# Second attention stage: order of SyncE's transfers, place of the inversion of head sums, and scaling of results in one group

## The chip, the cores and the metric

The kernel runs on one core of a Trainium2 chip. The metric is device time in microseconds of one execution of the whole program, the median of several runs. TensorE (PE) multiplies matrices, VectorE (DVE), ScalarE (ACT) and GpSimd (POOL) compute elementwise, SyncE (SP) only issues transfers (DMAs) between HBM and the on-chip memory SBUF; PE writes to the accumulator memory PSUM.

## What is computed

Two transformer layers over x of 8 x 512 tokens with 256 features. Layer 0 adds an attention with softmax and a feed-forward network. Layer 1, the one at hand, adds a linear attention and a feed-forward network of 8 experts, of which each token takes 2:

```python
q = x @ Wq.T; k = x @ Wk.T; v = x @ Wv.T            # 16 heads of 16 features
q = elu(q) + 1.0
k = elu(k) + 1.0
kv_cumsum = cumsum(einsum('blhd,blhe->blhde', k, v), axis=1)
k_cumsum = cumsum(k, axis=1)
out = einsum('blhd,blhde->blhe', q, kv_cumsum)
normalizer = clip(einsum('blhd,blhd->blh', q, k_cumsum), 1e-06, None)
out = (out / normalizer[..., None]).reshape(b, l, HIDDEN) @ Wo.T
```

## The kernel before

Four stages run one after the other: `stage_f` and `stage_a` for layer 0, `stage_b` for the linear attention and the gating of layer 1, `stage_c` for the experts. All that follows is `stage_b`. Each engine has a program of its own, written by hand; engines wait for one another on counting semaphores, and the order on each engine is the order of its code.

The stage handles 8 batches (B = 8) of 512 tokens, each in 4 tiles of 128 tokens (t = 0 to 3). The loop over b on every engine is a software pipeline: in pass b the scores, masks and states of batch b are made, the queries, keys and values of batch b+1 (`make(b + 1, t)`: t=0 the transposed input, t=1 the queries, t=2 the keys, t=3 values, gates and expert choice), and the results of batch b-1 are scaled, projected and added. Pass 7 makes nothing new, pass 8 only finishes batch 7.

On DVE, in each tile of a pass: `mask(b, t)` (L1632) takes the scores from PSUM, `take_state(b, t)` (L1646) the new part of the state; then come the `make` parts: `x_low` (L1617), `feature("q")` and `feature("k")` (L1624), `weigh_experts` and `choose`. A feature needs PE's product and ScalarE's exponential (`b_ex`, L1786), and it frees a PSUM bank. PE, ACT and DVE hand the two banks `pG` from use to use in a fixed sequence, and in it `project_out(b-1, 0)` takes the bank of the first key feature and `project_out(b-1, 1)` that of the second.

The normalizer comes as a row of ones beside the values: the results `o` hold sums of heads in rows 16, 48, 80 and 112. To invert them on all partitions they go on a round trip through HBM, all from SP's queue: the sums from `o` to `dens` (L1396), `dens` to the tile `den` (128 x 64, L1398), DVE's `invert` (clamp L1652, reciprocal L1654), `den` to `invs` (L1400), and `invs` four times to `inv_rows` (L1405). `normalise(b, t)` (L1659), called a scaling below, multiplies a tile of `o` by a tile of `inv_rows`, both in SBUF. `project_out` (PE, L1537) needs it; `add_out` (DVE, L1664) adds the product to `x_t`, and SP stores `x_t` when the last `add_out` of the batch is done (`store`, L1410). `x_t` has 4 buffers, so `load(b + 2)` (L1390) waits until `store(b - 2)` has landed. SP issues transfers in the order of its code and stands still at each wait.

GpSimd in each pass: `add_state(b, 1)`, then `own_queries(b + 1)` (L1880, four operations TENSOR_SCALAR as soon as the query features are there), `add_state(b, 2)` (L1889), and between them the sends of rows to the experts (L1924). At the end of the stage it splits a first set of expert weights in four pieces (L1950), behind its last sends.

Of the kernel before, what the change touches and what calls it, by code (L numbers as in the profile page):

```python
# [34 lines left out]
B, S, D = 8, 512, 256  # L35
T = B * S
NT = S // P
# [100 lines left out]
def tokens(ap, b):  # L138

    return ap[bass.ds(b * S, S), :].rearrange("(t p) d -> p t d", p=P)  # L140
# [1084 lines left out]
def stage_b(nc, wq_t, wk_t, wvg_t, wo_t, bg, own2_d, causal_d, blocks_d, before_d, ident_d,  # L1225
# [11 lines left out]
    with ExitStack() as ctx:  # L1237
# [142 lines left out]
        def wait_read(eng, *what):  # L1380
            n = rounds[what]
            eng.wait_ge(round_read[n % 2], n // 2 + 1)

        with nc.Block() as block:
            @block.sync
            def _(sp):
# [2 lines left out]
                        sp.wait_ge(stored[b % RX], 16 * (b // RX))  # L1389
                    sp.dma_start(x_t[:, b % RX, :, :], tokens(x1, b)).then_inc(x_in[b % RX], 16)  # L1390

                def invert(b):


                    sp.wait_ge(o_out, NT * (b + 1))
                    sp.dma_start(dens[b % 2, :, :], o[16:P:32, b % 2, :, :].rearrange("j g q -> j (g q)")).then_inc(den_out, 16)  # L1396
                    sp.wait_ge(den_out, 16 * (b + 1))
                    sp.dma_start(den[:], dens[b % 2, :, :].rearrange("j (r e) -> (j r) e", e=64)).then_inc(den_in, 16)  # L1398
                    sp.wait_ge(inv_step, 2 * b + 2)
# [8 lines left out]
                def store(b):  # L1408
                    wait_read(sp, "out", b, NT - 1)
                    sp.dma_start(tokens(out, b), x_t[:, b % RX, :, :]).then_inc(stored[b % RX], 16)  # L1410
# [9 lines left out]
                load(1)  # L1420
                sp.dma_start(dispatch.raw[:], weights[0:P, :]).then_inc(dispatched, 16)
                for b in range(B + 1):
                    if b + 2 < B:
                        load(b + 2)
                    if b >= 1:
                        invert(b - 1)
                        if b == B:
                            store(b - 2)
                        if b != B - 1:
                            store(b - 1)  # L1430
                sp.wait_ge(dispatched, 16)
                sp.wait_ge(padded, 16 * (NE + 1))
                for i in range(RX):
# [154 lines left out]
            def _(dve):  # L1588
# [148 lines left out]
                for b in range(B + 1):  # L1737
                    for t in range(NT):
# [4 lines left out]
                        if t == 3 and b + 2 < B:  # L1743
                            norm(b + 2)
                        if b >= 1:
                            if t == 1:
                                invert(b - 1)
                            if t == 2:
                                for i in range(NT // 2):
                                    normalise(b - 1, i)  # L1750
                        if b + 1 < B:
                            make(b + 1, t)
                        if b >= 1 and t == 2:
                            for i in range(NT // 2, NT):
                                normalise(b - 1, i)
                        if b == B - 1 and t == 3:
                            count_tiles()
                        if b >= 1 and t >= 2:
# [615 lines left out]
```

## Time and profile before

| | us |
|---|---|
| median of 3 runs | 2083.79 |
| lowest, highest | 2082.50, 2087.86 |
| the profiled execution | 2079.97 |
| its span, first to last instruction | 2078.3 |
| PE, DVE, ACT, POOL busy | 1882.9, 1244.4, 931.8, 1270.1 |
| second attention, about | 1247 to 1600 |

The profile is that of one execution. A timeline row gives start, duration, engine, line, operation, tiles written and read; in brackets stands how long the engine idled before it and what ended the idle time. "x2" means that two such instructions in a row are shown as one. Matrix products of one line appear as many instructions, and ends on PE are modelled.

### The profile page before, as it was taken

The numbers are of one execution on the slowest core, as the hardware profiler recorded it, in microseconds if no ns is written. First come the engines' busy times: TensorE is split into PE (matmuls) and PEld (weight loads), VectorE is DVE, ScalarE is ACT, GpSimd is POOL, SyncE is SP. The second block draws the span as 40 slices with busy tenths as digits, with TensorE's granted clock in tenths as the row PEclk, the third lists the DMA queues.
The fourth block names the chain that finished last, engine by engine and source line by source line (L and its number), as shares of the span: only waits on it lengthen the run. The fifth ranks groups of instructions, "written<-read, shape, count | busy, mean of one in ns | idle before, by whom it ended". The sixth has DMA issues, their size and how long they took to land. (4 is left out here: it accounts for less than half of the span.)

```text
span 2078.3 us, 35394 instructions
## 1 busy us (share of the span) xinstructions
PE 1882.9 (91%) x12820; PEld 1311.8 (63%) x12820; DVE 1244.4 (60%) x1819; ACT 931.8 (45%) x1605; POOL 1270.1 (61%) x824
## 2 busy tenths in 40 slices
PE   6997799999999999999999976888883899998998
PEld 5887444544545454454544545676762899998998
DVE  5775466656565666656666525776763566656343
ACT  5885344334343433434334224433320456776554
POOL 3553588778687887868778643455463664435433
PEclk8999799999999999999999988999996899999999
DMA  4223322232231323213232202132224443332222
GB/s 138 102 107 113 107 58 64 50 96 62 72 82 31 92 62 84 62 38 92 52 102 52 62 32 105 41 96 68 72 67 148 133 86 81 85 77 53 37 47 42
DMA packets 82432, 158.35 MB, mean 76 GB/s; under 512 B 14680, under 2 KB 64088, under 8 KB 76496
## 3 DMA queue, kind: packets, MB, share of 16 engines
q1 hardware_dynamic: 64832, 130.50, 22.6%
q0 software_dynamic: 14592, 18.40, 5.6%
q10 hardware_dynamic: 2880, 7.73, 1.0%
q8 instruction: 82, 1.34, 0.3%
q14 instruction: 46, 0.38, 0.1%
HBM read 80.45 MB, written 44.15 MB: 60 GB/s over the span
## 5 line engine op out<-in xcount | busy, mean ns | idle before, releaser
L1162 ACT ACTIVATE a_pr<-a_pT 128x1024 f32<-128x1024 f32 x256 | 261.8, 1023 | 425.3 <-PE a_pT L940 425.3
L1195 POOL TENSOR_TENSOR a_total<-a_total,a_pr 128x1024 f32<-128x1024 f32 x128 | 320.6, 2505 | 148.9 <-ACT a_pr L1162 148.5
L1051 DVE TENSOR_REDUCE a_row_max<-a_pG 128x2 f32<-128x1024 f32 x256 | 309.1, 1220 | 144.6 <-PE a_pG L914 144.3
L953 PE MATMUL a_pA<-a_pr,a_v 128*64 128x512 f32 x1024 | 277.4, 620 | 0.1
L2154 DVE TENSOR_TENSOR c_h_lo<-c_h,c_h_hi 128x256 fp32r<-128x256 f32 x288 | 151.3, 532 | 181.3 <-ACT c_h_hi L2128 181.0
L2128 ACT ACTIVATE c_h<-c_pU,c_b_c 128x256 f32<-128x256 f32 x288 | 140.8, 489 | 177.9 <-PE c_pU L105 176.6
L1195 POOL TENSOR_TENSOR a_total<-a_pr 128x1024 f32<-128x1024 f32 x64 | 151.7, 2370 | 51.4 <-ACT a_pr L1162 51.1
L1176 POOL TENSOR_TENSOR a_by_cos<-a_by_cos,a_swapped 128x1024 f32<-128x1024 f32 x64 | 155.4, 2429 | 36.7 <-DMA a_swapped<-a_by_sin 36.6
L1183 POOL TENSOR_TENSOR a_qk_lo<-a_by_cos,a_qk_hi 128x1024 fp32r<-128x1024 f32 x64 | 158.7, 2480 | 2.3 <-ACT a_qk_hi L1130 2.3
L1045 DVE TENSOR_TENSOR a_by_sin<-a_pG,a_sin 128x1024 f32<-128x1024 f32 x64 | 78.3, 1224 | 129.4 <-PE a_pG L105 124.7
L2198 POOL DMA_INDIRECT out_x<-c_y,c_ids x72 | 118.0, 1639 | 40.8 <-DVE c_y L2168 24.1
L2128 ACT ACTIVATE c_h_hi<-c_pU,c_b_c 128x256 fp32r<-128x256 f32 x288 | 139.9, 486 | 0.0
L914 PEld LDWEIGHTS a_pG<-a_qk_hi 64*128 64x128 f32 x512 | 45.9, 186 | 143.7 <-issue 91.0
L914 PE MATMUL a_pG<-a_qk_hi 64*128 64x512 f32 x512 | 120.8, 489 | 5.1 <-ACT a_qk_hi L1130 3.8
L1130 ACT CAST a_qk_hi<-a_by_cos 128x1024 fp32r<-128x1024 f32 x64 | 67.0, 1046 | 110.3 <-POOL a_by_cos L1176 110.3
L103 PE MATMUL c_pU<-c_xT_hi,d_w_lo 128*128 128x256 f32 x368 | 108.8, 296 | 7.3 <-remote 6.2
L935 PE MATMUL a_pT<-a_qk_hi,a_qk_lo 64*128 64x512 f32 x512 | 113.2, 436 | 1.9 <-ACT a_pr L1162 1.7
L103 PE MATMUL c_pY<-d_w_hi,c_h_lo 128*128 128x256 f32 x368 | 105.5, 287 | 8.5 <-DVE c_h_lo L2154 8.3
L940 PE MATMUL a_pT<-a_neg_max,a_ones 64*128 64x512 f32 x512 | 108.9, 419 | 0.0
L104 PE MATMUL c_pU<-c_xT_lo,d_w_hi 128*128 128x256 f32 x368 | 106.7, 290 | 0.0
L105 PE MATMUL c_pU<-c_xT_hi,d_w_hi 128*128 128x256 f32 x368 | 105.9, 288 | 0.0
L953 PEld LDWEIGHTS a_pA<-a_pr,a_v 128*64 128x64 f32 x1024 | 50.8, 135 | 86.9 <-issue 85.9
(271 smaller groups left out, 4986.3 us busy)
## 6 DMA issues: line engine op xcount, KB each, us to landing
a_swapped<-a_by_sin SPq DMA_DIRECT2D x256, 128.0 KB, 2.3
a_inv_by_head<-mid_inverses SPq DMA_DIRECT2D x30, 512.0 KB, 5.8
c_x_t<-mid_rows SPq DMA_DIRECT2D x37, 272.0 KB, 2.9
mid_latents<-f_c_parts SPq DMA_DIRECT2D x8, 1024.0 KB, 3.9
a_latent_parts<-mid_latents SPq DMA_DIRECT2D x8, 1024.0 KB, 7.4
d_raw<-in_weights SPq DMA_DIRECT2D x3, 2048.0 KB, 8.2
c_raw<-in_weights SPq DMA_DIRECT2D x3, 2048.0 KB, 7.7
f_x_t<-in_x SPq DMA_DIRECT2D x8, 512.0 KB, 3.8
```

The costliest lines, as they stand in the source:

```text
L103: nc.tensor.matmul(out, l_lo, r_hi, start=start, stop=False, **kw)
L914: last = nc.tensor.matmul(pair[:, h, :], qk_hi[rows, u % RQ, 0, t * P:(t + 1) * P], qk_hi[rows, u % RQ, 1, :], start=True, stop=True)
L935: nc.tensor.matmul(pT[:, h, :], k[rows, 1, ks], q[rows, 0, :], start=(i == 0), stop=False)
L953: last = nc.tensor.matmul(pA[64 * h:64 * h + 64, :], v[:, t, p, h, :], pr[:, n % RP, h, :], start=(t == 0), stop=(t == NT - 1))
L1051: nc.vector.reduce_max(row_max[:, u % 2, :, t], pair[:], AX.X).then_inc(read, 1)
L1162: nc.scalar.activation(pr[:, n % RP, :, :], pT[:], ACT.Exp, scale=SCALE).then_inc(exp_done, 1)
L1176: nc.gpsimd.tensor_tensor(by_cos[:, u % 2, :, :], by_cos[:, u % 2, :, :], swapped[:], ALU.add).then_inc(rope_done, 1)
L1183: nc.gpsimd.tensor_tensor(qk_lo[:, u % RQ, :, :], by_cos[:, u % 2, :, :], qk_hi[:, u % RQ, :, :], ALU.subtract).then_inc(qk_lo_done, 1)
L1195: nc.gpsimd.tensor_tensor(total[:, u % 2, :, :], before, pr[:, n % RP, :, :], ALU.add).then_inc(summed, 1)
L2128: nc.scalar.activation(dst[:, m % RH, :], pU[m % RH][:], ACT.Relu, bias=b1_c[:, e, m:m + 1]).then_inc(relu_done[m % RH], 1)
L2154: nc.vector.tensor_tensor(h_lo[:, m % RH, :], h[:, m % RH, :], h_hi[:, m % RH, :], ALU.subtract).then_inc(h_lo_done[m % RH], 1)
L2198: pool.indirect_dma_start(out=out, out_offset=bass.IndirectOffsetOnAxis(ap=ids[:, t:t + 1], axis=0), in_=y[:, t, :], in_offset=None, compu ...
```

## The change

SP: the sending of sums becomes a function of its own, `send_sums`, and goes first in a pass; `store(b - 2)` follows it, then `invert(b - 1)`, then `load(b + 2)`. Before, a pass had `load(b + 2)`, the sums and `invert(b - 1)` together, then `store(b - 1)`. DVE: `invert(b - 1)` moves from t=1, ahead of the query features, to t=0, behind `x_low`; the four scalings of t=2 come in one group ahead of the key features, where two stood ahead of and two behind them. No instruction is added or taken out.

```diff
-                def invert(b):
-
+                def send_sums(b):
                     sp.wait_ge(o_out, NT * (b + 1))
                     sp.dma_start(dens[b % 2, :, :], o[16:P:32, b % 2, :, :]...).then_inc(den_out, 16)
+
+                def invert(b):
+
                     sp.wait_ge(den_out, 16 * (b + 1))
...
                 for b in range(B + 1):
+                    if b >= 1:
+                        send_sums(b - 1)
+                    if 2 <= b < B:
+                        store(b - 2)
+                    if b >= 1:
+                        invert(b - 1)
                     if b + 2 < B:
                         load(b + 2)
-                    if b >= 1:
-                        invert(b - 1)
-                        if b == B:
-                            store(b - 2)
-                        if b != B - 1:
-                            store(b - 1)
+                    if b == B:
+                        store(b - 2)
+                store(B - 1)
...
                         if b >= 1:
-                            if t == 1:
-                                invert(b - 1)
                             if t == 2:
-                                for i in range(NT // 2):
+                                for i in range(NT):
                                     normalise(b - 1, i)
                         if b + 1 < B:
                             make(b + 1, t)
-                        if b >= 1 and t == 2:
-                            for i in range(NT // 2, NT):
-                                normalise(b - 1, i)
+                        if b >= 1 and t == 0:
+                            invert(b - 1)
```

SP's queue in pass 3 before, from the load to the store at the pass's end:

```order
L1390 DMA b_x_t<-mid_x 128x4x256
L1396 DMA mid_dens<-b_o 4x2048
L1398 DMA b_den<-mid_dens 128x64
L1400 DMA mid_invs<-b_den 128x64
L1405 DMA b_inv_rows<-mid_invs 16x2048 x4
L1410 DMA out_x<-b_x_t 128x4x256
```

The same queue in pass 3 of the changed kernel (lines are 5 or fewer further down):

```order
L1395 DMA mid_dens<-b_o 4x2048
L1412 DMA out_x<-b_x_t 128x4x256
L1400 DMA b_den<-mid_dens 128x64
L1402 DMA mid_invs<-b_den 128x64
L1407 DMA b_inv_rows<-mid_invs 16x2048 x4
L1390 DMA b_x_t<-mid_x 128x4x256
```

The sums moved ahead of store and load, the store between the sums and the read of `den`, the load behind the inverse rows.

DVE's program in pass 3 before, from the first `take_state` to the end of t=2's `add_out`; `d_scores` is the mask's result, `b_state` and `b_part` are `take_state`'s:

```order
L1646 TENSOR_TENSOR b_state<-b_pS,b_blocks 128x512
L1617 TENSOR_TENSOR b_xT_lo<-b_pG,b_xT_hi 128x512 x2
L1632 TENSOR_TENSOR d_scores<-b_pA,b_causal 128x2048
L1646 TENSOR_TENSOR b_part<-b_pS,b_blocks 128x512
L1652 TENSOR_SCALAR b_den<-b_den 128x64
L1654 RECIPROCAL b_den<-b_den 128x64
L1624 SCALAR_TENSOR_TENSOR b_qT<-b_pG,b_ex 128x512 x2
L1632 TENSOR_TENSOR d_scores<-b_pA,b_causal 128x2048
L1646 TENSOR_TENSOR b_part<-b_pS,b_blocks 128x512
L1659 TENSOR_TENSOR b_o<-b_o,b_inv_rows 128x4x128 x2
L1624 SCALAR_TENSOR_TENSOR b_kT<-b_pG,b_ex 128x512 x2
L1659 TENSOR_TENSOR b_o<-b_o,b_inv_rows 128x4x128 x2
```

DVE's program at the same place of the changed kernel:

```order
L1651 TENSOR_TENSOR b_state<-b_pS,b_blocks 128x512
L1622 TENSOR_TENSOR b_xT_lo<-b_pG,b_xT_hi 128x512 x2
L1657 TENSOR_SCALAR b_den<-b_den 128x64
L1659 RECIPROCAL b_den<-b_den 128x64
L1637 TENSOR_TENSOR d_scores<-b_pA,b_causal 128x2048
L1651 TENSOR_TENSOR b_part<-b_pS,b_blocks 128x512
L1629 SCALAR_TENSOR_TENSOR b_qT<-b_pG,b_ex 128x512 x2
L1637 TENSOR_TENSOR d_scores<-b_pA,b_causal 128x2048
L1651 TENSOR_TENSOR b_part<-b_pS,b_blocks 128x512
L1664 TENSOR_TENSOR b_o<-b_o,b_inv_rows 128x4x128 x4
L1629 SCALAR_TENSOR_TENSOR b_kT<-b_pG,b_ex 128x512 x2
```

Clamp and reciprocal moved ahead of the mask of t=1, and the second pair of scalings ahead of the key features.

## Rows read from the trace of the kernel before

**Rows 1.** Table of stretches, pass 3: length, busy us (count) PE, PEld, DVE, ACT, POOL

```profile
1387.54:1424.93 37.39, 33.20 (x402) 26.28 (x401) 27.16 (x61) 13.82 (x29) 20.31 (x29) 1.00 0.29 76
```

**Rows 2.** Waits, 1353 to 1537 us: engine, who for whom, total, times, longest

```profile
PE b_pG L1537 <- DVE b_kT L1624: 14.0, 5, 3.5
```

**Rows 3.** Timeline of PE, pass 3 and pass 7: start, us, instruction, idle before

```profile
1397.84 1.15 PE L1487 MATMUL b_pA<-d_own,b_kT 32*128 32x256 f32 x16
...
1408.14 3.72 PE L1537 MATMUL b_pG<-b_wo,b_o 128*128 128x256 f32 x16 [2.62 <-DVE b_kT L1624]
...
1554.56 5.07 PE L1537 MATMUL b_pG<-b_wo,b_o 128*128 128x256 f32 x16 [4.58 <-DVE b_o L1659]
```

**Rows 4.** Timeline of DVE, pass 3, instructions apart

```profile
1392.17 2.29 DVE L1632 TENSOR_TENSOR d_scores<-b_pA,b_causal 128x2048 f32<-128x2048 f32 x1 [0.56 <-PE b_pA L1487]
...
1397.08 0.19 DVE L1652 TENSOR_SCALAR b_den<-b_den 128x64 f32<-128x64 f32 x1 [2.02 <-DMA b_den<-mid_dens]
...
1401.33 0.68 DVE L1646 TENSOR_TENSOR b_part<-b_pS,b_blocks 128x512 f32<-128x512 f32 x1
...
1405.77 1.11 DVE L1659 TENSOR_TENSOR b_o<-b_o,b_inv_rows 128x512 f32<-128x512 f32 x1 [3.76 <-DMA b_inv_rows<-mid_invs]
```

**Rows 5.** Timeline of SP's queue, passes 2 and 3, then passes 7 and 8

```profile
1387.65 0.40 SPq L1410 DMA_DIRECT2D out_x<-b_x_t  x1
...
1391.06 0.50 SPq L1396 DMA_DIRECT2D mid_dens<-b_o  x1
1395.21 0.34 SPq L1398 DMA_DIRECT2D b_den<-mid_dens  x1
1397.89 0.34 SPq L1400 DMA_DIRECT2D mid_invs<-b_den  x1
1399.37 2.33 SPq L1405 DMA_DIRECT2D b_inv_rows<-mid_invs  x4
...
1537.15 0.50 SPq L1396 DMA_DIRECT2D mid_dens<-b_o  x1
...
1546.88 3.32 SPq L1405 DMA_DIRECT2D b_inv_rows<-mid_invs  x4
1564.95 0.50 SPq L1396 DMA_DIRECT2D mid_dens<-b_o  x1
```

**Rows 6.** Timeline of ACT: last copy of batch 2's results; first key exponential

```profile
1382.80 0.57 ACT L1812 COPY b_o<-b_pO 128x512 f32<-128x512 f32 x1
...
1403.78 0.64 ACT L1786 ACTIVATE b_ex<-b_ex 128x512 f32<-128x512 f32 x1
```

**Rows 7.** Timeline of POOL, pass 3: own queries and `add_state`

```profile
1398.90 6.19 POOL L1880 TENSOR_SCALAR d_own<-b_qT,b_own 128x512 f32<-128x512 f32 x4
1405.07 1.26 POOL L1889 TENSOR_TENSOR b_state<-b_state,b_part 128x512 f32<-128x512 f32 x1
```

**Rows 8.** Timelines of DVE and POOL: scalings of passes 1, 6; first stage

```profile
1329.63 0.92 DVE L1659 TENSOR_TENSOR b_o<-b_o,b_inv_rows 128x512 f32<-128x512 f32 x1 [1.60 <-DMA b_inv_rows<-mid_invs]
1330.47 2.19 DVE L1659 TENSOR_TENSOR b_o<-b_o,b_inv_rows 128x512 f32<-128x512 f32 x1
...
1517.43 2.54 DVE L1659 TENSOR_TENSOR b_o<-b_o,b_inv_rows 128x512 f32<-128x512 f32 x1 [2.33 <-DMA b_inv_rows<-mid_invs]
...
77.89 1.19 POOL L338 TENSOR_SCALAR f_diag<-f_ident,f_rstd 128x128 f32<-128x128 f32 x1
78.61 0.77 DVE L528 TENSOR_TENSOR f_g_lo<-f_g,f_g_hi 128x512 fp32r<-128x512 f32 x1
```

**Rows 9.** Timelines of DVE, POOL and PE, passes 7 and 8

```profile
1553.72 2.63 DVE L1659 TENSOR_TENSOR b_o<-b_o,b_inv_rows 128x512 f32<-128x512 f32 x4 [4.37 <-DMA b_inv_rows<-mid_invs]
...
1567.45 9.23 POOL L1950 TENSOR_TENSOR d_w_lo<-d_raw,d_w_hi 128x1024 fp32r<-128x1024 f32 x4
...
1570.25 6.48 DVE L1652 TENSOR_SCALAR b_den<-b_den 128x64 f32<-128x64 f32 x1 [1.87 <-DMA b_den<-mid_dens]
...
1585.76 9.98 PE L1537 MATMUL b_pG<-b_wo,b_o 128*128 128x256 f32 x32 [17.84 <-DVE b_o L1659]
```

## The prediction

> **What bounds the kernel now.** I read the views from coarse to fine. The change touches only the second attention, from about 1247 to 1600 us. The table of stretches [rows 1] shows one pass of its loop, from the first mask of one batch to that of the next: 37.39 us with TensorE (PE) busy for 33.20 and VectorE (DVE) for 27.16. So PE bounds a pass, and some 4 us of it are not PE's. The view of waits over passes 2 to 6 [rows 2] names most of them: PE waited 14.0 us in five times for a key feature of DVE, 3.5 us the longest. I call the pass with loop value b "pass b"; pass 3 starts at 1387.54 us and stands for passes 2, 5 and 6.
>
> In pass 3 the timelines tell what is late. PE is idle for 2.62 us and starts `project_out(2,0)` at 1408.14 [rows 3], so it was free at 1405.52. That product needs the bank that the first key feature frees, and this feature stands on DVE behind two scalings of results (L1659), which wait 3.76 us for the inverse rows until 1405.77 [rows 4]. The rows are late because of SyncE: the sums were complete when ScalarE ended its copy at 1382.80 + 0.57 = 1383.4 [rows 6], but SP stood in `store(1)` until 1387.65, then waited with the next load for that store to land, and only then sent the sums, at 1391.06 [rows 5]. The other wait, 2.02 us before the clamp of `den` [rows 4], is on nobody's path: the mask behind it needs `scores(3,2)`, which PE ends at 1397.84 + 1.15 = 1398.99 [rows 3], later than DVE could be there.
>
> **SP's new order.** The sums go at about 1383.5. `store(1)` stays at 1387.65, since it waits for the last `add_out`. The read of `den` follows at 1388.1 instead of 1395.21, but behind 512 KB of store. A read alone needs 1.87 us (1395.21 to its use at 1397.08); the sums behind a load took 4.15 (1391.06 to 1395.21) [rows 4, 5]. So `den` lands between 1390.0 and 1392.3; I take the middle, 1391.1. The load of `x_t` goes behind the inverse rows, to about 1395.7. Its reader comes behind `project_out`, which ends at 1411.86 [rows 3] and would now end some 2.6 us earlier: 13 us of cover for one transfer, so it costs nothing. The last two stores keep their place.
>
> **Invert at t=0.** Clamp, reciprocal and SP's answer took 1397.89 - 1397.08 = 0.81 us. They go ahead of the mask of t=1 at 1392.17, where DVE idles 0.56 us for PE anyway [rows 4], from 1391.6 on. They delay that mask by 0.2 us, by 0.9 at the late bound of `den`. Queued behind it are `take_state` and through it GpSimd's `add_state` and own queries, which move by the same 0.2 us; `scores(3,2)` on PE needs the mask only at 1397.84. The inverses leave at 1392.4 instead of 1397.89, their rows 1.48 us later, at 1393.9 [rows 5]. Issue to use took 6.4 us here (1399.37 to 1405.77) and 6.8 in pass 7 (1546.88 to 1553.72) [rows 4, 5, 9]. So they are there by 1400.3 to 1401.4 with the late `den` too. DVE comes to use them after `take_state`, at 1401.33 + 0.68 = 1402.0 [rows 4]. The wait of 3.76 us goes.
>
> **Four scalings in one go.** Alone, four of them take 2.63 us [rows 9]: 1402.0 to 1404.6. The first exponential of the keys ends at 1404.42 [rows 6], its feature at 1405.3 with the 0.65 us that such an operation takes (2.63 / 4), and PE, free at 1405.52, waits for nothing: a gain of 2.6 us, the most there is. But the scalings now fall among GpSimd's four own queries (1398.90 to 1405.09) and its `add_state` (1405.07 to 1406.33) [rows 7], and a scaling reads two SBUF tiles. What that costs is the unknown of this change. The rows that bear on it: in pass 3 the first scaling met `add_state` and took 1.11 instead of some 0.68 us [rows 4]. In pass 1 one that started in the last own query took 0.92 and the next, which met `add_state`, 2.19; in pass 6 one that started in the last own query took 2.54, until `add_state` was over [rows 8]. In the first stage, where GpSimd runs four of the same kind of operation (TENSOR_SCALAR), a DVE operation with two SBUF inputs took 0.77 us, and it was GpSimd's that stretched, to 1.19 [rows 8]. I read this as: own queries let DVE in after 0.1 to 0.5 us, `add_state` does not. Then the four scalings pass before `add_state` with some 0.7 us of delay in all, the first key feature ends at 1402.0 + 2.6 + 0.7 + 0.65 = 1405.95, and PE gains 2.1 us instead of 2.6. Passes 2, 3, 5, 6: 4 x 2.1 = 8.4. Pass 4 lost 3.5 us in the same place [rows 2] and comes down to the same pattern: 3.0. In pass 1 the scalings come later among the own queries: 0.5. Together 11.9 us. After PE everything moves along, since DVE's chain of t=3 starts from `project_out`.
>
> **The end of the stage.** Pass 7 makes nothing new, so nothing covers its inverse rows: scalings at 1553.72, PE idle 4.58 us, `project_out` 5.07 us instead of 3.72 [rows 3, 9]. New: the read of `den` takes the place of the sums at 1537.15 [rows 5], lands by 1540.2, and the inverse rows leave at about 1542.8 instead of 1546.88. They land at 1549.4, and with some 1 us for the `add_state` of that pass the first scaling ends 3.3 us earlier than now. With the short idle PE's 16 products take 3.72 again, and the last copy of results comes 4.6 us earlier: the sums leave at 1560.3 instead of 1564.95. Here the gain grows. The clamp of the last batch takes 6.48 us now (1570.25 to 1576.7), the very time until GpSimd ends four splits of weights (1567.45 to 1576.68) [rows 9], and these do not move: they stand behind GpSimd's own sends. With the sums 4.6 us earlier the clamp comes at 1565.6, before the splits. The inverse rows go at 1568.0, land 6.4 to 7.5 us later, and the scalings meet the last split, which ends at 1576.7. PE starts at about 1577.3 instead of 1585.76 [rows 9]: 8.5 us. If a scaling slips in between splits it is 10.5.
>
> **Sum.** 11.9 + 8.5 = 20.4 us off the profiled execution's 2079.97: 2059.6. The median of the three runs lies 3.8 us above it (2083.79), so 2063.4.
>
> **Rivals.** (a) Taking turns: a scaling waits for GpSimd's operation in progress, and GpSimd's next goes ahead of the next scaling. Two scalings pass before `add_state`, two behind it (from 1406.2): first key feature at 1408.1, as now. The passes gain nothing, the end keeps 8.5: 2075.3. (b) Blocked throughout, as the 2.54 us scaling of pass 6 was: four scalings from 1406.2, first key feature at 1406.2 + 2.6 + 0.65 = 1409.45, 1.3 us later than now in passes 2, 3, 5, 6, some 2.0 in pass 1, 0.4 in pass 4: +7.6, minus 8.5: 2082.9. The Trainium skill, "SBUF — State Buffer", Who interferes with whom, speaks against the change here: a VectorE instruction with two SBUF inputs and a GpSimd instruction that reads SBUF exclude each other for a whole instruction, and the later one fully blocks. By that rule, with turns of 1.55, 1.55 and 1.26 us between the scalings, the key feature would end at about 1409.5, the same time as (b). The rows of 1.11, 2.19 and 2.54 us agree with it, those of 0.92 and 0.77 do not [rows 4, 8]. (c) Slower: the block in both places. The passes lose 7.6 us, and the last `den` lands after 1567.45, when the first split has begun; the clamp then stays blocked until 1576.7 and the whole gain of the end is gone, since the splits do not move. It takes 1.9 us of delay against my chain: 2091.4. (d) The passes gain, the end misses that moment: 2071.9. (e) No collision at all and a scaling between splits: 2057.
>
> **How the numbers follow.** Forecast 0.45, (a) 0.20, (b) 0.13, (c) 0.07, (d) 0.10, (e) 0.05. A measurement here tells about 0.3%, 6.3 us, from no change: faster is below 2077.5. The forecast, (d), (e) and most of (a), whose bound is 2 us away, lie there: 0.72. (b) and the rest of (a) lie within: 0.20. (c) and a sliver of (b) are slower: 0.08. The range goes from 2057, the best case, to 2084, just past (b).
>
> **What would show it.** The sums issued within 1 us of ScalarE's last copy; no wait of DVE for `den` over 0.5 us; scalings right behind `take_state` in passes 1 to 6; their durations: 0.7 to 1.2 us each (forecast), two of 1.5 or more (a), the first over 4 (b). PE's wait for a key feature at 0.5 us per pass instead of 2.62. The last clamp at 0.2 instead of 6.48 us. I am wrong if a pass stays at 37.4 us though the wait for inverse rows is gone, or if the last clamp still meets the splits.

## The result, and the profile after

Beside the kernel before (2084.92 us, 20 runs) the changed kernel took **2087.65 us** (20 runs, 2083.19 to 2098.01). The ratio is 1.0018, 95% interval 1.0011 to 1.0026: 0.2% slower and no gain, where 2063.4 was forecast. Its profiled execution took 2087.03 us, with a span of 2085.4; that of before had 2078.3.

The table of stretches of the changed kernel: one pass (3), then passes 1 to 6 together, then pass 7 until the last `add_out` starts.

```profile
core 0: us, PE busy (x) PEld busy (x) DVE busy (x) ACT busy (x) POOL busy (x), PEclk, DMA share, GB/s
1388.33:1428.05 39.72, 35.02 (x402) 27.57 (x401) 29.32 (x62) 13.94 (x29) 21.21 (x29) 0.96 0.29 72
...
1308.49:1545.24 236.75, 205.96 (x2389) 161.46 (x2390) 173.15 (x346) 79.49 (x169) 128.05 (x173) 0.97 0.27 68
1545.24:1603.23 57.99, 35.73 (x354) 26.98 (x353) 22.32 (x32) 6.32 (x9) 28.50 (x30) 0.79 0.43 117
```

Pass 3 is 2.33 us longer than in [rows 1]. The same stretches of before are 225.20 and 58.59 us. So the passes lost 11.5 us and the end gained 0.6; the stages ahead were 3.5 us shorter in this execution and those behind 0.3: 11.5 - 0.6 - 3.5 - 0.3 = 7.1, the difference of the two spans. The place is inside the passes. (The trace of before is a short one: with 2079.97 us its execution lies below the lowest of the 20 runs, 2082.50, and its passes are 3 us shorter than in e13 and e17, two later traces of the same kernel.) The timelines of pass 3, by engine (SP, PE, POOL, ACT, DVE); line numbers have moved by 2 to 5 against before:

```profile
1384.18 0.50 SPq L1395 DMA_DIRECT2D mid_dens<-b_o  x1
1394.78 1.71 SPq L1407 DMA_DIRECT2D b_inv_rows<-mid_invs  x4
...
1397.65 1.08 PE L1532 MATMUL b_pO<-d_scores,b_v 128*32 128x128 f32 x32
1401.01 1.08 PE L1506 MATMUL b_pO<-b_qT,b_state 128*32 128x128 f32 x32 [1.21 <-ACT b_o L1814]
1409.55 5.41 PE L1542 MATMUL b_pG<-b_wo,b_o 128*128 128x256 f32 x16 [1.92 <-DVE b_kT L1629]
...
1398.68 0.97 POOL L1926 DMA_INDIRECT mid_rows<-b_xm,b_slots  x1 [0.31 <-issue]
1404.34 2.52 POOL L1882 TENSOR_SCALAR d_own<-b_qT,b_own 128x512 f32<-128x512 f32 x1
1406.83 1.50 POOL L1891 TENSOR_TENSOR b_state<-b_state,b_part 128x512 f32<-128x512 f32 x1
...
1400.28 0.59 ACT L1814 COPY b_o<-b_pO 128x512 f32<-128x512 f32 x1 [1.27 <-remote]
...
1400.51 2.29 DVE L1637 TENSOR_TENSOR d_scores<-b_pA,b_causal 128x2048 f32<-128x2048 f32 x1 [0.72 <-PE b_pA L1492]
1403.80 1.11 DVE L1664 TENSOR_TENSOR b_o<-b_o,b_inv_rows 128x512 f32<-128x512 f32 x1
1404.83 0.68 DVE L1664 TENSOR_TENSOR b_o<-b_o,b_inv_rows 128x512 f32<-128x512 f32 x1
1405.43 1.78 DVE L1664 TENSOR_TENSOR b_o<-b_o,b_inv_rows 128x512 f32<-128x512 f32 x1
1407.13 1.76 DVE L1664 TENSOR_TENSOR b_o<-b_o,b_inv_rows 128x512 f32<-128x512 f32 x1
1408.81 0.68 DVE L1629 SCALAR_TENSOR_TENSOR b_kT<-b_pG,b_ex 128x512 f32<-128x512 f32 x1
```

What the change is for has happened: the sums go within 1 us of ScalarE's copy, the inverse rows 6.45 us into the pass instead of 11.83 [rows 5], and no scaling waits for them in passes 1 to 6. Two things take the place of that wait.

1. **TensorE's results come late at t = 1.** `weigh(3,1)` starts at 1397.65, so it should be through at 1398.73; ScalarE's copy of `o` starts only at 1400.28, `from_state` waits 1.21 us for it, the mask of t = 2 waits 0.72 us. In the trace of before nothing of this shows: the same copy starts 10.56 us into the pass, here 11.95. The scalings therefore start 15.47 us into the pass instead of 14.4.
2. **The four scalings take 5.09 us**, 2.50 in passes 7 and 8. The first waits inside an own query, the second passes (and GpSimd's next one stretches to 2.52), the third waits for that one, the fourth for `add_state`.

So the key feature starts 20.48 us into the pass (19.87 in before) and PE idles 1.92 us. In passes 1, 3 and 4 its 16 products then take 5.41 instead of 3.72 us, with a mean granted clock of 0.68 (part of them at the 1.2 GHz level); in passes 2, 5 and 6, behind the same idle time, they run at 1.00, the 2.4 GHz level, and take 3.72. The end lost its gain in another way; these rows of PE, POOL, ACT and DVE are of passes 7 and 8:

```profile
1569.21 0.98 PE L1532 MATMUL b_pO<-d_scores,b_v 128*32 128x128 f32 x23 [1.67 <-DVE d_scores L1637]
...
1574.11 0.41 PE L1532 MATMUL b_pO<-d_scores,b_v 128*32 128x128 f32 x1 [0.78 <-issue]
...
1574.51 0.97 POOL L1926 DMA_INDIRECT mid_rows<-b_xm,b_slots  x1 [0.30 <-issue]
...
1577.21 0.59 ACT L1814 COPY b_o<-b_pO 128x512 f32<-128x512 f32 x1 [18.53 <-remote]
...
1582.39 1.14 DVE L1657 TENSOR_SCALAR b_den<-b_den 128x64 f32<-128x64 f32 x1 [2.12 <-DMA b_den<-mid_dens]
```

The last `weigh`, 1.08 us elsewhere, takes 5.3, and the last copy comes 8.0 us after its start (1.1 in before), 1.7 us after the last of eight sends in a row. The last clamp is short (1.14 us, where 0.2 was hoped for and before had 6.48), but late.

### The profile page after: what moved, and what is told of

The parts are those of the page before. It is cut to its first block and busy times, and to the rows that moved or that the text cites. A ratio compares the mean times of both kernels' runs of the same rounds, so it can differ in the third digit from the quotient of the medians.

```text
span 2085.4 us, 35394 instructions
## 1 busy us (share of the span) xinstructions
PE 1886.8 (90%) x12820; PEld 1313.0 (63%) x12820; DVE 1252.0 (60%) x1819; ACT 932.6 (45%) x1605; POOL 1276.0 (61%) x824
## 5 line engine op out<-in xcount | busy, mean ns | idle before, releaser
L1195 POOL TENSOR_TENSOR a_total<-a_total,a_pr 128x1024 f32<-128x1024 f32 x128 | 325.2, 2541 | 145.4 <-ACT a_pr L1162 144.6
L1195 POOL TENSOR_TENSOR a_total<-a_pr 128x1024 f32<-128x1024 f32 x64 | 151.7, 2371 | 49.6 <-ACT a_pr L1162 49.4
```

Source lines behind the costliest of these rows:

```text
L1195: nc.gpsimd.tensor_tensor(total[:, u % 2, :, :], before, pr[:, n % RP, :, :], ALU.add).then_inc(summed, 1)
```

## The experiments

A **sitting** is what was run together: one chip, each kernel in turn with the kernel before. One plain fact is needed to read the numbers: the unedited changed kernel gives one of two times, and all runs of a sitting give the same one (2078.79 to 2098.01 us in three sittings, 2058.63 to 2064.94 in two). In **late** sittings (the first result, e9, e10 to e12) TensorE's results come late as above; in **prompt** ones (e1 to e4, e5 to e8, e13 to e16, e17 and e18) they don't. The expectations say slow and quick for these.

| run | kernel | sitting | us, median | ratio to before (95%) | passes 1 to 6 | pass 7 to last `add_out` |
|---|---|---|---|---|---|---|
| - | before, profile of [rows 1] | copies prompt | 2084.92 | 1 | 225.2 | 58.6 |
| - | changed | late | 2087.65 | 1.0018 (1.0011-1.0026) | 236.8 | 58.0 |
| e9 | changed | late | 2085.82 | 0.9998 (0.9987-1.0009) | 235.6 | 56.6 |
| e10 | changed | late | 2082.60 | 0.9991 (0.9978-1.0004) | 234.6 | 57.4 |
| e6 | changed | prompt | 2064.01 | 0.9910 (0.9889-0.9931) | 211.2 | 49.4 |
| e14 | changed | prompt | 2061.24 | 0.9901 (0.9874-0.9928) | 210.0 | 57.4 |
| e1 | own queries last | prompt | 2067.32 | 0.9928 (0.9910-0.9945) | 214.3 | 56.7 |
| e2 | scalings 2 + 2 | prompt | 2063.87 | 0.9910 (0.9889-0.9929) | 209.0 | 57.9 |
| e11 | scalings 2 + 2 | late | 2071.46 | 0.9944 (0.9922-0.9966) | 217.6 | 57.5 |
| e12 | sends late | late | 2067.28 | 0.9924 (0.9903-0.9945) | 210.6 | 57.8 |
| e3 | SyncE's order only | prompt | 2078.60 | 0.9980 (0.9967-0.9992) | 225.6 | 54.8 |
| e4 | rows held | prompt | 2109.86 | 1.0130 (1.0107-1.0154) | 258.2 | 56.6 |
| e8 | grouping only | prompt | 2095.64 | 1.0068 (1.0047-1.0088) | 241.8 | 58.6 |
| e5 | 2 + 2, splits held | prompt | 2055.32 | 0.9865 (0.9841-0.9889) | 209.1 | 51.2 |
| e7 | changed, splits held | prompt | 2055.83 | 0.9868 (0.9841-0.9896) | 210.8 | 49.6 |
| e16 | e5 and sends late | prompt | 2055.81 | 0.9876 (0.9857-0.9896) | 209.1 | 51.4 |
| e15 | e16 and last sends held | prompt | 2057.74 | 0.9881 (0.9863-0.9900) | 209.1 | 51.2 |
| e18 | as e15 | prompt | 2056.58 | 0.9881 (0.9864-0.9898) | 208.9 | 51.5 |
| e13, e17 | before | prompt | 2082.57, 2081.86 | 0.9997, 0.9998 | 228.2, 228.6 | 57.3, 58.8 |

The last two columns are read from each profile: start of the first mask of pass 1, of pass 7, and of the last `add_out`. The kernels of the experiments had 2 (e14) to 12 runs. The kernel before took 2081.4 to 2082.8 us in the prompt sittings, 2083.8, 2084.9 and 2086.0 in the late ones.

### One cause at a time: e1 to e4

e1 puts `own_queries` behind `add_state(b, 2)` and the scalings; e2 undoes the grouping; e3 keeps SyncE's order and undoes everything on VectorE; e4 holds the inverse rows.

```
# e1, GpSimd                              # e2, VectorE, t == 2
-if b + 1 < B:                            -for i in range(NT):
-    own_queries(b + 1)                   +for i in range(NT // 2):
 add_state(b, 2)                               normalise(b - 1, i)
+if b + 1 < B:                             if b + 1 < B:
+    if b >= 1:                                make(b + 1, t)
+        pool.wait_ge(norm_done, NT * b)  +if b >= 1 and t == 2:
+    own_queries(b + 1)                   +    for i in range(NT // 2, NT):
                                          +        normalise(b - 1, i)
# e3: e2, and invert(b - 1) ahead of the make of t == 1, as before
# e4, SyncE, ahead of the four inverse rows
+if b + 1 < B:
+    sp.wait_ge(masked, NT * (b + 1) + 3)
```

> The changed kernel with GpSimd's four own-query multiplications of the next batch moved behind add_state(b, 2) and behind a wait for the four scalings, so that scalings and own queries no longer run side by side. Theory A (shared access: in passes 1 to 6 the four scalings took 5.05 to 5.12 us beside the own queries, 2.50 without them in passes 7 and 8): the group takes about 2.6 us, the first key feature starts 2.5 us sooner, VectorE's group and GpSimd's (7.16 us) go back to 2.6 and 6.2, PE's wait for the key features' buffer (about 1.9 us a pass) goes, and the kernel comes to 2074 to 2080 us. Rival B (the loss is in TensorE's results that come late ahead of the scalings, and in the clock): the group is short but the time stays within 2 us of the changed kernel's 2087.7. Rival C (the gain comes back as a wait): add_state, sends and slots move 6 us later and the next pass waits for them, 2085 or more.

> The changed kernel with the scalings again two ahead of the key features and two behind them; SyncE's order and the place of the clamp as changed. Theory A: only two scalings (about 2.2 to 2.6 us beside GpSimd) stand ahead of the key features, the first key feature starts about 2.5 us sooner, PE's 1.9 us wait ahead of project_out goes, the other two scalings hide behind the key features; 2074 to 2080 us. Rival B (late results of TensorE, clock, end of the stage): within 2 us of 2087.7. The end of the stage has no own queries beside the scalings and is the same in both theories.

> SyncE's new order alone: VectorE clamps and inverts at t = 1 and scales two and two, as in the kernel before. Theory A: sums reach VectorE early and wait there for the clamp at the old place (8.7 us into a pass), so the inverse rows land at most 2 us sooner than before; the passes gain 0 to 1 us each, the end of the stage what it gains; 2078 to 2084 us. On the late results of TensorE: if the early inverse rows' transfers (in flight 6 to 13 us into a pass in the changed kernel) are their cause, ScalarE's copy of o at t = 1 comes 1.3 us after the start of weigh here, as before, since the rows are sent 4 us later; if the sums or the store are the cause, it comes 2.6 us after, as in the changed kernel.

> The changed kernel, but SyncE sends the inverse rows only once mask(b, 2) of the pass is done (about 14 us into it instead of 6.5). A cost of its own is meant: the scalings then wait for rows that land at about 20 us, 3 to 5 us a pass, 2100 to 2120 us. What it tells: theory R (the inverse rows' transfers in flight make TensorE's weigh and scores end late at t = 1): ScalarE's copy of o at t = 1 comes 1.3 us after weigh starts and mask(b, 2) does not wait. Rival (their cause is the order of VectorE's work, or the sums and the store): 2.6 us and 0.7 us as in the changed kernel.

e1 and e2 came out 0.7 and 0.9% faster than before and seemed to prove theory A. But their passes of 35.5 to 35.9 and 34.7 us were better than the theory allowed, and in passes 2 to 6 of all four traces the copy at t = 1 started 10.54 to 10.56 us into the pass: what was to be explained was not there. Beside the prompt changed kernel (e6, e14, further down) e2 is no quicker and e1 is 3 to 6 us slower. Three results stand by themselves. SyncE's order alone (e3) leaves the inverse rows to land 16.4 to 17.3 us into the pass instead of some 18.2, for 0.2%. e2 differs from e3 only in the place of `invert`, t = 0 instead of t = 1, and is 14.7 us quicker: with SyncE's order in place, this edit brings most of the gain. Rows that land at 20.0 to 22.6 (e4) cost 1.3%: PE idles 5.3 to 6.3 us in each pass, at a mean clock of 0.89 to 0.92.

### The changed kernel again: e5 to e9

e5 is e2 with GpSimd's splits held; e7 is the changed kernel with that edit alone; e8 is the kernel before with the four scalings grouped (e2's edit the other way round); e6 and e9 are the changed kernel, unedited.

```
# e5, e7: GpSimd, ahead of the four splits
+pool.wait_ge(inv_step, 2 * B)
```

> The kernel with the scalings two and two (2063.9 us in its run), and GpSimd's splits of the stage behind held back until VectorE has inverted the last sums. There the last clamp took 7.57 us of a span of VectorE that is 0.20 us in other passes, with four back-to-back splits of GpSimd (9.22 us) beside it. Theory (the splits lock the clamp out and it is on the path to the last inverse rows): the clamp takes 0.2 us, the last scalings start 7.4 us sooner, the stage ends 7 us sooner, 2055 to 2059 us. Rival (the splits are wanted in time by the stage behind, or its loads set its start): the clamp is short, but at least half of the 7 us comes back as a wait in the next stage, 2060 to 2064.

> The changed kernel once more, unedited, beside the other kernels of this call. It is to tell what in its profile repeats. Theory G (the group of four beside GpSimd is what costs): the scalings again take about 5.1 us a pass, the key features come 2.4 us later than with two and two, PE waits 1.9 us, and the kernel is 1.0 to 1.3% slower than with two and two. Open: whether TensorE's weigh(b, 1) again ends 1.3 us late in each pass, and whether its last weigh again takes until 8 us after its start. If both are gone and the time is the same within 2 us, they were of one execution; if they come again, they belong to the kernel.

> The changed kernel (four scalings in a group) with GpSimd's last splits held back until the last sums are inverted, and no other edit. Theory (the end is a stretch of its own, whatever the passes do): 5 to 7 us less than the changed kernel beside it, the last clamp 0.2 us. Rival (in the changed kernel the splits already came late, behind ScalarE's last copy, and the clamp took 1.14 us): 0 to 2 us.

> The kernel before with all four scalings in one group ahead of the key features and nothing else changed. The inverse rows land 18.1 us into a pass, when GpSimd's own queries are through but add_state(b, 2) (1.26 us) is not. Theory A (the grouping costs by itself): the key features start 1.2 to 1.5 us later, seven passes 8 to 10 us, 0.4 to 0.5% slower than before. Rival (grouping costs only beside the own queries): within 0.15% of before.

> The changed kernel, unedited, a second time, in a call of its own. Its result beside the kernel before was 2087.65 us (20 runs) and in a later run of the same program 2064.0 us (6 runs): both medians stand, and the passes of the two traces differ by 4 us each at the same order of work. In the slow trace TensorE is late only where GpSimd issues its sends at the same time (weigh(b, 1) at 9.3 us into a pass beside sends at 9.1 to 11.3 us; the last weigh beside eight sends, in steps of 0.71 us); in the quick one it is not, with the same sends. Theory C (what made it late belonged to that chip or to how the program lay in memory there): again 2059 to 2067 us. Rival (it comes and goes from load to load of this program): 2083 to 2098 us, with the copy of o at t = 1 again 2.6 us after the start of weigh.

**e6 took 2064.01 us, e9 2085.82.** Stretches and timelines of e6 (pass 3; passes 1 to 6 together; pass 7 on):

```profile
1387.81:1422.64 34.83, 33.23 (x402) 26.31 (x401) 27.33 (x62) 13.81 (x29) 20.93 (x29) 1.00 0.34 82
...
1526.38:1575.79 49.41, 30.56 (x354) 23.79 (x353) 21.28 (x33) 6.31 (x9) 28.58 (x30) 0.86 0.50 137
1315.21:1526.38 211.17, 199.12 (x2389) 157.38 (x2390) 162.06 (x346) 79.06 (x169) 125.47 (x173) 0.99 0.31 76
```

```profile
1397.10 1.08 PE L1532 MATMUL b_pO<-d_scores,b_v 128*32 128x128 f32 x32
...
1398.17 0.97 POOL L1926 DMA_INDIRECT mid_rows<-b_xm,b_slots  x1 [0.30 <-issue]
1402.27 2.56 POOL L1882 TENSOR_SCALAR d_own<-b_qT,b_own 128x512 f32<-128x512 f32 x1
...
1398.37 0.57 ACT L1814 COPY b_o<-b_pO 128x512 f32<-128x512 f32 x1
...
1402.20 0.68 DVE L1664 TENSOR_TENSOR b_o<-b_o,b_inv_rows 128x512 f32<-128x512 f32 x1
1402.80 0.69 DVE L1664 TENSOR_TENSOR b_o<-b_o,b_inv_rows 128x512 f32<-128x512 f32 x1
1403.40 1.18 DVE L1664 TENSOR_TENSOR b_o<-b_o,b_inv_rows 128x512 f32<-128x512 f32 x1
1404.51 0.68 DVE L1664 TENSOR_TENSOR b_o<-b_o,b_inv_rows 128x512 f32<-128x512 f32 x1
1405.11 0.68 DVE L1629 SCALAR_TENSOR_TENSOR b_kT<-b_pG,b_ex 128x512 f32<-128x512 f32 x1
...
1405.84 3.72 PE L1542 MATMUL b_pG<-b_wo,b_o 128*128 128x256 f32 x16
```

Up to `weigh(3,1)`, 9.3 us into the pass, the two traces of the same program agree within 0.04 us in every row of PE, DVE and POOL (the copy at t = 0 alone is 0.24 us later in the late one, and the inverse rows go 0.2 us later). Then the copy comes 10.56 us into the pass against 11.95. The scalings start at 14.39 against 15.47, and that moment decides their price: here two slip past the third own query before it gets in (it is the one that stretches, to 2.56), the third waits half a microsecond, and the fourth is through before `add_state` (1406.59). The group takes 2.98 us, and PE does not idle before `project_out`. Pass 3 is 4.89 us shorter than in the late trace: `project_out` starts 3.19 us sooner (18.03 against 21.22 us into the pass) and is 1.69 us shorter.

e8 goes the way of theory A and further than its 8 to 10 us: 14.3 us slower than before. No further collision is needed for it. In passes 2, 3 and 5 the first scaling is held until `add_state` is through, as in before; then three more follow at 0.6 us each instead of one, so the key feature starts at 21.1 us instead of 19.87. PE idles 3.85 us (5.35 in pass 4) where [rows 2] has 3.5 at most, and the products then run at a mean granted clock of 0.67 to 0.71 in five of six passes:

```profile
1414.10 2.37 PE L1537 MATMUL b_pG<-b_wo,b_o 128*128 128x256 f32 x7 [3.85 <-DVE b_kT L1624]
```

So in the order of before, the grouping alone costs 0.7%; it is SyncE's earlier rows together with `invert` at t = 0 that make it harmless, in a prompt sitting.

**The end of the stage** is settled by e5 and e7. These are the last splits and the last clamp in e14 (the changed kernel, prompt), then in e7:

```profile
1551.48 9.22 POOL L1952 TENSOR_TENSOR d_w_lo<-d_raw,d_w_hi 128x1024 fp32r<-128x1024 f32 x4
...
1553.01 7.75 DVE L1657 TENSOR_SCALAR b_den<-b_den 128x64 f32<-128x64 f32 x1 [1.85 <-DMA b_den<-mid_dens]
```

```profile
1556.18 4.63 POOL L1953 TENSOR_TENSOR d_w_lo<-d_raw,d_w_hi 128x1024 fp32r<-128x1024 f32 x2 [1.04 <-DVE b_den L1659]
...
1555.31 0.20 DVE L1657 TENSOR_SCALAR b_den<-b_den 128x64 f32<-128x64 f32 x1 [2.18 <-DMA b_den<-mid_dens]
```

In e14 the clamp meets the splits by 1.5 us and ends when they end. In e6's profile it is 0.9 us ahead of them and takes 0.20 us. That end is 8 us shorter, and that execution (2058.98 us) is the shortest of e6's six. Its clamp also came 1.9 us sooner than e14's, so some 6 us of the 8 are the splits'. It came sooner as the first 16 products of pass 7 took 3.69 us behind 1.65 us of idle time in e6 and 5.38 behind 2.13 in e14, at a mean granted clock of 1.00 and 0.68. With the splits held the clamp is short each time: e7 is 8.2 us below e6 in the same sitting, and the end of e5 is 6.7 us shorter than that of e2, which has the same scalings 2 + 2 and the same slow products (5.38 us). The next stage does not miss the splits.

### What makes TensorE's results late: e10 to e12

```
# e12, GpSimd
 add_state(b, 1)
-if b >= 1:
-    send(b - 1, 2)
 if b + 1 < B:
     own_queries(b + 1)
 add_state(b, 2)
 if b >= 1:
+    send(b - 1, 2)
     send(b - 1, 3)
```

> The changed kernel, unedited, as the control of this call: on this chip either near 2064 us (as e6) or near 2087 us (as its first result and e9). It says in which of the two ways the neighbours of this call are to be read. The two slow results came with no other kernel beside the kernel before, the quick one with three others: if the company decides, it is quick here; if the chip decides, either.

> Scalings two and two, again. Where the control is quick: as e2, 2060 to 2066 us. Where it is slow, theory G (TensorE's late weigh moves the scalings from 14.4 to 15.4 us into a pass, where the group of four meets own queries and add_state and takes 5.1 us; with two ahead the meeting costs one turn): 2068 to 2076, well under the control; rival (the lateness of TensorE is the cost, the grouping only follows it): within 4 us of the control.

> The changed kernel with GpSimd's two sends of tile 2 issued behind add_state(b, 2), next to those of tile 3, instead of beside weigh(b, 1). Where the control is slow, theory S (TensorE's late results at t = 1 come from GpSimd's sends at that time together with the inverse rows in flight): the copy of o at t = 1 starts 10.56 us into the pass instead of 11.92, mask(b, 2) at 11.6 instead of 12.2, and the kernel takes 2062 to 2070 us; rival (the inverse rows' transfers alone, or anything that is not the sends): the copy stays at 11.9 and the time within 4 us of the control. Where the control is quick it shows nothing on this; the own queries then start 1.2 us sooner and free the scalings' last turn: 2060 to 2064.

The control e10 was late, so the sitting tells. It had the chip of e1 to e4, which were prompt: the chip does not decide, nor does the company of other kernels. Pass 4 gives a comparison inside the late traces, as VectorE was some tenths later or earlier there. The rows are `weigh(4,1)`, one of the two sends of tile 2 (the second in e9, the first in e10) and the copy:

```profile
1442.33 1.08 PE L1532 MATMUL b_pO<-d_scores,b_v 128*32 128x128 f32 x32
...
1444.01 0.97 POOL L1926 DMA_INDIRECT mid_rows<-b_xm,b_slots  x1 [0.30 <-issue]
...
1445.55 0.58 ACT L1814 COPY b_o<-b_pO 128x512 f32<-128x512 f32 x1 [1.85 <-remote]
```

```profile
1441.55 1.08 PE L1532 MATMUL b_pO<-d_scores,b_v 128*32 128x128 f32 x32
1442.56 0.99 POOL L1926 DMA_INDIRECT mid_rows<-b_xm,b_slots  x1 [0.16 <-issue]
...
1443.13 0.59 ACT L1814 COPY b_o<-b_pO 128x512 f32<-128x512 f32 x1 [0.22 <-PE b_pO L1532]
```

In e9 the `weigh` ends, at 1443.41, while the two sends run (1442.72 to 1444.98), and its copy starts 0.57 us after they end; in pass 3 of the first result it was 0.63 (1399.65 to 1400.28). In e10 the sends begin as `weigh` ends, and the copy follows 0.5 us behind it (0.2 in prompt traces), before they are through; that pass takes 36.68 us, its scalings 3.27, where the passes around it take 39.69 (1.7 us of it at the lower clock) and 5.12. Two more places of the late traces agree. At t = 0 of pass 3 of the first result the sends end 3.11 us into the pass and the copy starts at 3.73, 0.62 us later; in pass 7, where no send runs as the `weigh` of t = 1 or of t = 2 ends, both copies come as in prompt traces, at 8.13 and 12.86 us. And e12, with the sends moved, in the same late sitting:

```profile
1393.15 1.08 PE L1532 MATMUL b_pO<-d_scores,b_v 128*32 128x128 f32 x32
...
1394.42 0.57 ACT L1814 COPY b_o<-b_pO 128x512 f32<-128x512 f32 x1
...
1398.25 2.90 DVE L1664 TENSOR_TENSOR b_o<-b_o,b_inv_rows 128x512 f32<-128x512 f32 x4
...
1546.69 1.08 PE L1532 MATMUL b_pO<-d_scores,b_v 128*32 128x128 f32 x32 [1.47 <-DVE d_scores L1637]
...
1553.57 0.97 POOL L1926 DMA_INDIRECT mid_rows<-b_xm,b_slots  x1 [0.30 <-issue]
...
1555.93 0.58 ACT L1814 COPY b_o<-b_pO 128x512 f32<-128x512 f32 x1 [19.38 <-remote]
```

The copy at t = 1 is prompt (10.57 us into the pass), the group takes 2.90 us, a pass 34.87, and the kernel is 15.3 us below its control. The copy at t = 0, where sends remain, starts at 3.71 us as in every late trace (3.49 in prompt ones). That is shown: in a late sitting, what TensorE finishes beside GpSimd's sends is seen 0.6 us after the sends. The end of the stage is late in e12 too: the last copy 9.2 us after its `weigh` starts and 1.4 us after the last of eight sends.

e11 separates the two parts of the loss. With the copy as late as in e10 (11.9 us), but only two scalings ahead of the key features, a pass takes 36.0 us and the kernel is 11.1 us below the control; the group itself, not the lateness alone, is what costs most.

### Does the kernel before hide the same: e13 to e18

e16 is e5 with e12's edit; e15 and e18 also hold the last six sends until ScalarE's last copy (`pool.wait_ge(o_out, NT * B)` ahead of them); e13 and e17 are the kernel before, e14 the changed one.

> The kernel before, unedited, profiled beside the changed kernel. Theory S (in some sittings what TensorE finishes while GpSimd issues sends is seen only when the sends are through; the kernel before hides it, since its scalings wait for the inverse rows anyway): in a sitting in which the control shows the copy of o at 11.9 us, here too the copy comes at about 11.9 and mask(b, 2) at 12.2 instead of 10.56 and 11.58, but the rows' landing moves by less than 0.5 us and the pass is 37.4 to 38 us long. Rival (the lateness needs the changed order, its early inverse rows in flight): the copy stays at 10.56 while it is late in the control. In a sitting where the control is quick it says nothing.

> The changed kernel, unedited, the control of this sitting: 2059 to 2067 us with the copy of o at 10.56 us into a pass and the last copy 0.2 us after the last weigh, or 2080 to 2090 us with 11.9 us and 8 us or more.

> Scalings two and two, sends of tile 2 behind add_state(b, 2), the splits held until the last sums are inverted, and the last six sends held until ScalarE's last copy of o. Theory S: no send is beside a weigh whose result is on the path, so it takes the same in either sitting: passes of 34.7 to 34.9 us, stage end as in the run with the splits held, 2052 to 2058 us. Rival (the held sends and splits then reach past the stage's end and the next stage waits): 2058 to 2066 us.

> The same without holding the last six sends. Theory S: equal to the kernel with four edits within 2 us where the control is quick; where it is slow, 7 to 9 us slower than that one, since the last weigh's result waits for eight sends. Rival (what the last copy waits for is not the sends): equal within 2 us in both.

> The kernel before, unedited, profiled once more, since the last sitting was a quick one. The sitting is told by the copy of o at t = 0 of a pass, in this kernel and in its neighbour: 3.49 us into the pass in quick sittings, 3.7 in slow ones. If it is a slow one, theory S: the copy at t = 1 at 11.9 us and mask(b, 2) at 12.2 instead of 10.56 and 11.58, the last copy (of the stage) over 7 us after the last weigh's start, but the inverse rows land as before (17.5 to 18.5 us) and hide the first of these; 2083 to 2088 us. Rival: the copies at 3.49 and 10.56 while the neighbour's are late. In a quick sitting: 2081 to 2084 us, nothing told.

> The kernel with four edits (scalings two and two, sends of tile 2 behind add_state(b, 2), splits held, last six sends held). Quick sitting: 2055 to 2060 us as in e15. Slow sitting, theory S: the copy at t = 1 at 10.6 us, the last copy 1.2 us after the last weigh's start, 2055 to 2062 us, since no send is beside a weigh that is waited for. Rival: what is late in a slow sitting is not bound to the sends, and it takes 2066 us or more.

Both sittings were prompt (control 2061.24; copies at 3.48 and 10.55 in e13 and e17), so the question stays **open**: no trace of the kernel before is known to be from a late sitting. The record doesn't say in which sitting the trace of [rows 1] was taken. Its copies are prompt, and its execution is not among the 20 runs of the first result, while each other trace is one of its kernel's runs. If it was taken beside them after all, it speaks for the rival of e13, that the lateness needs the changed order. What bounds it: before lost 1 to 4.6 us from prompt to late sittings, the changed kernel 18.6 to 26.4. Open too is whether holding the last sends repairs the end in a late sitting; in prompt ones it costs 1 to 2 us against e16, within their spread. And nothing here says what makes a sitting late. In the three late ones the changed kernel stood first beside the kernel before, in the prompt ones it did not; that is a coincidence to try, not a cause.

**The best versions** are e5, e7 and e16, all at 0.987 to 0.988 of before, in prompt sittings. None was run in a late one, but e12 and e11 bear on it: scalings 2 + 2 and the sends out of the way of `weigh(b, 1)` are what held there. I would take e16.

## Why the prediction was wrong

**What bounds the kernel, and SP's new order**: right. In the traces the sums leave within 1 us of the last copy, `den` holds up the mask of t = 1 in pass 4 only, in e1 and e14 in pass 5 too, by up to 1.4 us, and in passes 1 to 6 of the changed kernel the rows are there before they are wanted.

**When the scalings can start**: the step that failed. "DVE comes to use them after `take_state`, at 1402.0", 14.4 us into the pass, holds in prompt sittings (14.39) and in e12. In the first result it was 15.47, since TensorE's `weigh` and `scores` beside GpSimd's sends were seen late. I had read the start from the trace of before, where that lateness does not show, and no row of it could have told me.

**The price of the group**: the forecast was 0.7 us of delay in all; e6 and e14 show 0.48 (2.98 against 2.50). That reading, "own queries let DVE in after 0.1 to 0.5 us, `add_state` does not", held there, and it hung on being ahead of `add_state`, with 1.4 us to spare in the prompt trace. One microsecond later rival (a) applies, turns with two scalings stretched to 1.8 us, and the key feature ends 21.16 us into the pass, where (a)'s 1408.1 is 20.6. I had priced the collision at one phase only. The Trainium skill's page "SBUF — State Buffer", Who interferes with whom, has a VectorE instruction with two SBUF inputs and a GpSimd instruction that reads SBUF exclude each other for a whole instruction. For `add_state` the traces agree: in the first result the fourth scaling, 0.68 us when alone, took 1.76 and ended 0.56 us behind `add_state`. But the third scaling of e6 ended at 1404.58, inside an own query that is recorded until 1404.83, so for that kind of instruction the measurement decides against it.

**The passes**: 11.9 us forecast. Prompt, against the trace of [rows 1]: 15.2 in e14 and 14.0 in e6, as PE's idle time before `project_out` went to nothing where I had left 0.5 us per pass, and pass 4 gave 3.4 to 3.5. Against e13, in e14's own sitting, it is 18.2. In [rows 1]'s trace the first 16 products of no pass from 1 to 6 fell to the lower clock; in e13 those of passes 3 and 4 did, in e17 those of 4 and 5, and their passes 1 to 6 took 3.0 and 3.4 us more. I had forecast from an execution that was spared this. Late: a loss of 11.5. It is the later start of `project_out` (0.5 to 0.6 us a pass, 1.2 in pass 1: 4.2 in all), 1.7 us of lower clock in each of passes 1, 3 and 4 (5.1), and some 0.75 us at t = 3 in passes 2, 5 and 6 (2.2), where the products of values begin 1 us before the last two sends of the pass end; in passes 1, 3 and 4 they begin behind them and nothing is lost there.

**The end**: 8.5 us forecast, on "these do not move: they stand behind GpSimd's own sends". The splits do move, since those sends belong to pass 7 and start as it does: 29.4 us into it in e14, 30.3 in before. The clamp, 30.9 us into it, met them by 1.5 us. This was rival (d), the passes gain and the end misses, and e14's end gains 1.2 us against [rows 1]'s trace and nothing against e13's. In e6 the clamp won that race by 0.9 us. The forecast also had the first 16 products of pass 7 back at 3.72 us; they took 5.38 in the first result and in e14, behind 2.05 and 2.13 us of idle time. In late sittings the end gains 0.6 to 2 us for another reason, the eight sends.

So the medians of 2064.0 and 2061.2 us in the prompt sittings agree with 2063.4 only in part by merit: against the trace of [rows 1] the passes gave 2 to 3 us more than forecast and the end usually 7 less, while the kernel before was itself 1 to 2.4 us below the 2083.79 from which the forecast was scaled. The chance of 0.28 on "same or slower" was for collisions; the range ended at 2084, just past (b), and left out (c), the only rival that was slower. The first result has (c)'s shape, passes that lose and an end that gives nothing, but neither part came by (c)'s way, and no case had a cause outside the trace of before.

## What to carry to other kernels

Price a collision between two engines at more than one phase: the same four scalings cost 0.5 us starting at 14.4 and 2.6 us starting at 15.5, and putting only two of them ahead of the work that the bottleneck waits for made the kernel 11 us less sensitive. A short operation that everything waits for must not be able to meet a row of long ones on the engine that it collides with; one wait that lets it go first was worth 8 us in the medians of e6 and e7. When a result contradicts a sum whose every other term checks out, run the same program again in another sitting before explaining it.

## What the runs showed of the hardware, unexpected

- Two levels of the same program, 2061 to 2064 and 2083 to 2088 us, constant within a sitting; one chip had a prompt sitting (e1 to e4) and a late one (e10 to e12).
- In late sittings a TensorE result that falls beside GpSimd's indirect sends is seen 0.6 us after the last of them at t = 1 (1.4 to 1.7 us behind a row of eight, with TensorE's weight loads in steps of 0.7 us in the first result). A copy whose `weigh` ends beside no send is not late (t = 2, and t = 1 and 2 of pass 7).
- A VectorE clamp of 0.2 us took 6.2 to 9.0 us beside four splits of GpSimd (before, e1, e2, e8, e13, e14, e17): it ended only with the fourth. In those runs the splits followed the last send at once. Where they began behind a wait of 0.25 to 3.3 us (e3, e4 and all late traces) the clamp was through as the second split ended, after 0.5 to 1.1 us. Why is not shown.
- TensorE's granted clock fell behind idle time. In all traces, the first 16 products of `project_out` in a pass took 5.1 us or more (mean clock 0.54 to 0.72) behind 3.84 us of idle time and more, sometimes so behind 1.9 to 3.5 us (passes 1, 3, 4 of the first result, not 2, 5 and 6, with the same idle time), and 3.7 us at a clock of 1.00 behind 1.8 us or less.
